# A macaron transformer block on one core: the ring of fetched expert rows gets eight places instead of four

## What is computed

```python
x = x + 0.5 * ffn(layernorm(x), gate_w, gate_up_proj, down_proj)
x = x + attn(layernorm(x), w_qkv, w_out)
x = x + 0.5 * ffn(layernorm(x), gate_w, gate_up_proj, down_proj)

def ffn(x):                       # 16 experts, each token goes to the best 2
    p = sigmoid(x @ gate_w.T); p = p / p.sum(-1)
    w, idx = top_k(p, 2);      w = w / w.sum(-1)
    # expert e: (silu(x @ gate_e) * (x @ up_e)) @ down_e, 256 -> 128 -> 256
    # out = sum of the two experts' outputs, weighted with w
```

## Time and profile before

| | |
|---|---|
| median of 3 runs | 817.87 us (816.4 to 819.97) |
| the profiled execution, whole | 817.24 us |
| its span, first to last instruction | 815.4 us |
| TensorE clock granted, mean of the span | 0.929 |
| busy, share of the span | PE 82%, PEld 65%, DVE 65%, ACT 51%, POOL 51% |
| chain that ended last, by engine | PE 62%, DVE 17%, issue 5%, DMA 4%, ACT 4%, POOL 2% |
| indirect fetches of line 1356 | 80, together 76.9 us busy on POOL |

### The profile page before, as it was taken

The page is one execution under the profiler, slowest core; times in us unless marked ns, Lnnn a source line. Parts: engine busy times, 40 slices in busy tenths (PEclk is TensorE's granted clock), DMA queues, the critical chain, the costliest instruction groups (busy, mean ns, idle before and its releaser), DMA issues.

```text
span 815.4 us, 17364 instructions
## 1 busy us (share of the span) xinstructions
PE 665.5 (82%) x5367; PEld 530.3 (65%) x5384; DVE 528.8 (65%) x1644; ACT 418.3 (51%) x1024; POOL 417.1 (51%) x557
## 2 busy tenths in 40 slices
PE   2638999887868999999999899896775656998990
PEld 2438889776746777777777566664434546887880
DVE  7888644333666888788888988855486313343678
ACT  1534566555414555555555555555564524565660
POOL 4124555555342555455555542357677674555551
PEclk9958999999978999999999999999877787999996
DMA  8793456555553444444444333246115343555979
GB/s 255 246 295 96 137 159 170 155 137 144 136 152 100 117 119 121 119 117 112 116 119 114 98 87 86 74 139 204 60 69 173 100 153 123 153 146 145 308 260 325
DMA packets 96920, 121.04 MB, mean 148 GB/s; under 512 B 12352, under 2 KB 83280, under 8 KB 96848
## 3 DMA queue, kind: packets, MB, share of 16 engines
q1 hardware_dynamic: 82992, 81.82, 33.5%
q0 software_dynamic: 13824, 38.29, 16.2%
q10 hardware_dynamic: 32, 0.02, 0.0%
HBM read 51.99 MB, written 38.34 MB: 111 GB/s over the span
## 4 chain that ended last, share of the span: by engine, by line
PE 62%; DVE 17%; issue 5%; another core or an unknown queue 4%; DMA 4%; ACT 4%; POOL 2%; SPq 2%; DVEq 0%; ACTq 0%; POOLq 0%
PE bank L1208 9%; PE bank L1516 8%; PE bank L613 6%; PE bank L1220 5%; PE bank L1523 4%; PE bank L674 4%; PE bank L635 4%; PE bank L660 4%; PE bank L694 3%; DVE mx L1020 3%; PE bank L620 3%; PE bank L1198 2%; PE bank L638 2%; PE bank L1507 2%
## 5 line engine op out<-in xcount | busy, mean ns | idle before, releaser
L525 POOL TENSOR_SCALAR_AFFINE_SELECT pr<-pr 128x512 f32<-128x512 f32 x128 | 81.4, 658 | 135.6 <-ACT pr L790 132.5
L1020 DVE TENSOR_REDUCE mx<-bank 128x2 f32<-128x512 f32 (+1 forms) x192 | 127.7, 683 | 29.6 <-PE bank L638 21.7
L790 ACT ACTIVATE pr<-bank 128x512 f32<-128x512 f32 x192 | 105.8, 603 | 40.0 <-PE bank L660 22.6
L1356 POOL DMA_INDIRECT spare<-normed,source x80 | 76.9, 962 | 89.4 <-PE bank L1507 43.6
L1166 POOL DMA_INDIRECT returned<-shared,source x80 | 77.5, 969 | 62.4 <-DVE shared L1296 41.7
L1208 PE MATMUL bank<-xeT,shared 128*128 128x128 f32 x640 | 90.0, 286 | 10.8 <-ACT xeT L1261 6.8
L1208 PEld LDWEIGHTS bank<-xeT,shared 128*128 128x128 f32 x640 | 82.7, 202 | 12.3 <-issue 12.0
L1516 PE MATMUL bank<-xeT,shared 128*128 128x128 f32 x640 | 87.6, 281 | 1.2 <-ACT xeT L1643 1.0
L1516 PEld LDWEIGHTS bank<-xeT,shared 128*128 128x128 f32 x640 | 80.6, 198 | 2.1 <-issue 2.0
L1289 DVE TENSOR_TENSOR act_rows<-bank,act_rows 128x128 f32<-128x128 f32 x80 | 23.2, 290 | 89.0 <-ACT act_rows L1277 55.3
L432 POOL DMA_INDIRECT gathered_rows<-grouped,slot x64 | 67.4, 1053 | 16.1 <-issue 12.3
(11 more groups left out here) (344 smaller groups left out, 1496.3 us busy)
## 6 DMA issues: line engine op xcount, KB each, us to landing
shared<-parts SPq DMA_DIRECT2D x154, 128.0 KB
grouped<-pr SPq DMA_DIRECT2D x80, 132.0 KB
spare<-grouped SPq DMA_DIRECT2D x80, 132.0 KB
spare<-parts SPq DMA_DIRECT2D x70, 128.0 KB
shared<-returned SPq DMA_DIRECT2D x32, 256.0 KB
normed<-shared SPq DMA_DIRECT2D x8, 512.0 KB, 3.9
wgu_sb<-_L_ffn_gate_up_proj_dram SPq DMA_DIRECT2D x8, 512.0 KB, 8.7
wd_sb<-in_L_ffn_down_proj_dram SPq DMA_DIRECT2D x8, 512.0 KB
```

The lines of the kernel that those rows point to most:

```text
L525: nc.gpsimd.affine_select(out=m, in_=m, compare_op=ALU.is_ge, fill=0.0, base=0, pattern=[[0, 4], [1, P]], channel_multiplier=-1).then_inc( ...
L790: nc.scalar.activation(dst.rearrange("p h n -> p (h n)"), bank[n % 3][:, :], ACT.Exp).then_inc(at["exp_ready"], 1)
L1020: nc.vector.tensor_reduce(mx[:, u, h0:h0 + nh], bank[3 + n % 2][:, :].rearrange("p (h k) -> p h k", h=nh), AX.X, ALU.max).then_inc(at["max ...
L1356: nc.gpsimd.indirect_dma_start(xe[r], None, normed, bass.IndirectOffsetOnAxis(source[:, j:j + 1], 0)).then_inc(xe_loaded[r], 16)
```

## The change

`AHEAD_X` = 8 replaces the four places: `xe` becomes the first 2048 columns of `spare`, with eight semaphores `xe_loaded`. The fetch of tile j waits for the transposes of tile j-8. As four of the places now lie where `wqk_in` lay, the fetch of tile 0 also waits until ACT has copied the q and k weights. PE's loop goes round eight tiles, in 8 iterations instead of 16, so that each place's address and semaphore are constants. The last block, which uses the same semaphores for the first of its 16 places, counts from the new totals. The ring of results `ye`, the loops of ACT, DVE and SP, and the place and number of the gathers are as before.

```diff
--- before.py
+++ after.py
@@ -43,6 +43,7 @@
     DUMP = TOPK * WIDE[2] * P
     ID_0 = [DUMP + (NE_T + TOPK * WIDE[1]) * P, DUMP + NE_T * P, 0]
     NK = NE_T // RING
+    AHEAD_X = 2 * RING
     LOADS = 4
     LATE = 6
     ROUNDS = NT // RING
@@ -207,7 +208,7 @@
         gathered_rows = sb("gathered_rows", [P, RING, TOPK, W])
         got = [[gathered_rows[:, r, k, :] for k in range(TOPK)] for r in range(RING)]
         before_in, source_in, passed_in = (bank[3], bank[5]), (bank[5], bank[4]), (bank[7], bank[5])
-        xe = [spare[:, (RING + r) * H:(RING + r + 1) * H] for r in range(RING)]
+        xe = [spare[:, r * H:(r + 1) * H] for r in range(AHEAD_X)]
         xeT = sb("xeT", [P, 2, HC, P])
         att = xeT[:, :, :, :].rearrange("p u c n -> p u (c n)")
         act_rows = sb("act_rows", [P, 2, 2, I])
@@ -303,10 +304,10 @@
         att_consts = sem("att_consts")
         first_block = {n: sem(f"{n}_f") for n in first_names}
         last_block = {n: sem(f"{n}_l") for n in last_names}
-        xe_loaded = [sem(f"xe_loaded{r}") for r in range(RING)]
+        xe_loaded = [sem(f"xe_loaded{r}") for r in range(AHEAD_X)]
         xl_loaded = [sem(f"xl_loaded{r}") for r in range(PLACES_X)]
         scattered = [sem(f"scattered{a}") for a in range(1, CLASSES)]
-        yl_returned = xe_loaded + [sem(f"yl_returned{r}") for r in range(RING, PLACES_Y)]
+        yl_returned = xe_loaded + [sem(f"yl_returned{r}") for r in range(AHEAD_X, PLACES_Y)]
         ye_stored = [sem(f"ye_stored{r}") for r in range(RING)]
         xn_stored = [sem(f"xn_stored{i}") for i in range(BACK)]
         late_loaded = (ye_stored + xn_stored)[0:LATE]
@@ -329,7 +330,7 @@
 
         def returns(r, n):
 
-            return 16 * (len(range(r, n, PLACES_Y)) + (NE_T // RING if r < RING else 0))
+            return 16 * (len(range(r, n, PLACES_Y)) + (NE_T // AHEAD_X if r < AHEAD_X else 0))
 
         count = [0]
 
@@ -1350,9 +1351,11 @@
 
             def fetch(j):
 
-                r = j % RING
-                if j >= RING:
-                    pool.wait_ge(s["xe_transposed"], j - RING + 1)
+                r = j % AHEAD_X
+                if j >= AHEAD_X:
+                    pool.wait_ge(s["xe_transposed"], j - AHEAD_X + 1)
+                elif j == 0:
+                    pool.wait_ge(at["wqk_ready"], 2 * HC)
                 nc.gpsimd.indirect_dma_start(xe[r], None, normed, bass.IndirectOffsetOnAxis(source[:, j:j + 1], 0)).then_inc(xe_loaded[r], 16)
 
             def stored_up_to(n):
@@ -1496,7 +1499,7 @@
                 place_tokens(k)
             passed_row(0)
 
-            body = RING
+            body = AHEAD_X
             alone = SURE - 1
             loops = (NE_T - alone - 1) // body
```

## The result

The changed kernel took 831.57 us (median of 4 runs, 826.4 to 833.09), the kernel before, on the same chip, 818.92 us (4 runs): ratio 1.015, interval 1.011 to 1.019. It is slower, by 12.7 us in the medians. The forecast was 823.5 and slower; the sign was right, and so in the main was the mechanism, but the size was half of what came.

A forecast was written before the change was run, and what follows sets the result against it. PE bounds the steady part; elsewhere POOL's back-to-back indirect DMAs delay reports of PE's work. Terms +1.9, +4.67 and -0.3 sum to +6.3 on 817.24, giving 823.5 us; range 809 to 832, the forecast alone 819.5 to 828.

The forecast's parts named there:

- the sign: Whole kernel: slower, 823.5 us against a profiled 817.24; slower was given 0.52, same 0.30, faster 0.18.
- the mechanism: First block's expert tiles: while POOL issues indirect DMAs back to back, PE's finished work is told late and everything stands.
- The wait at the head: Before the first fetch: waiting for ACT's q and k weight copies, over at 46.1 before the fetch at 55.04, costs nothing.
- the loop of eight: PE's loop over expert tiles: same instructions, half the branches, already hidden; 0, with a bound of -0.6 us.
- The start: 55 to 75 us: 15 fetches in a row cost 0, as a run of four did and DVE's routing sets the end.
- Rival C: Start: the run of 15 fetches hits DVE's routing chain, one standstill of 8 us on top, 831.5; chance 0.10.
- The pause for the list: Fetch 16, waiting for the list of all pairs: a run of at least five follows, +1.9 us, bounds 0 and 3.7.
- The first gathers: From 155.9 us: POOL's run grows from five to ten, 6.25 us more standing, 1.58 saved at gather 2: +4.67.
- the end: Last fetch of the expert tiles: issued eight tiles ahead, so the 0.3 us of waits for a fetch go: -0.3.
- Gathers 3 to 7: Later gathers among the fetches: each still costs 1.58 us as before, 6.2 us a step.
- Rival A: Stretch of the gathers: the ring is what stalls it, so more places make it faster, 811.8 to 802.3; chance 0.18.
- Rival B: Long waits come from the moment's traffic, not run length: no change, 816.9 to 818, at 817; chance 0.22.

The follow-up runs named there:

- the first experiment: The changed kernel with all its code, but the fetch of tile j waits for the transposes of tile j-4 as before: 816.48 us, ratio 0.9976 to the kernel before.

## Why the prediction was right, and where it was off

PE's first work on an expert tile, in the trace of before, bears on the second point:

```profile
60.55 1.03 PE L1507 MATMUL bank<-ident,spare 128*128 128x128 f32 x4
```

- **The wait at the head and the loop of eight: 0.** Right; the first experiment keeps both and loses nothing.
- **The start: 0, with 8 as the rival's price.** This is the step that failed: 4.3 us. I took the run of four at the start as showing that a run costs nothing here. It could not show that. The run is over at 59.33 + 0.95 = 60.28, and PE's first work on an expert tile starts only at 60.55, so there was no report of its tiles to be held. With eight places the run went on to 68.76, over PE's first tiles. It had eleven DMAs (15 had been forecast; the twelfth fetch waited for tile 3, whose report was held). Rival C had the mechanism and the place, at twice the price. The price does not follow from the length alone: the runs of five cost 5.4 us before the change and 3.0 at the list, the run of eleven 4.3. The rest of my reason for 0, that DVE sets the end here, did not cover it: DVE itself waits for ACT, and ACT for PE.
- **The pause for the list: +1.9.** The run of five came as forecast, and cost 3.0, inside the bounds of 0 and 3.7 and nearer to the row that had the same length.
- **The first gathers: +4.67, and the end: -0.3.** Run of ten in the forecast order; 4.6 us lost from tile 54 to 79 against the sum of 4.4. The single waits are shorter than the 8 to 10 us I expected, since they come in three pieces of 8.1 us together. The sum took its 6.25 us as standing still alone. Over tiles 54 to 60 idle time rose only from 4.8 to 8.1 us, and slower work at the lower clock from 2.3 to 4.5, so it is in part luck that the term came out so well. Gathers 3 to 7 cost 6.4 a step instead of 6.2.
- **Nothing between tile 14 and 54.** PE was 1.0 us quicker there.
- **Rival A (the ring frees the stretch of the gathers).** Wrong: POOL's runs got longer and PE's waits with them. **Rival B (the traffic of the moment).** Wrong on these chips: six DMAs of 4 KB did it in the steady stretch, and more traffic with pauses did not.

The forecast of 6.3 us stands against 9.2 in the profiled execution and 12.7 in the medians. Of the 2.9 us between forecast and profile, the start makes +4.3, the list +1.1, the first gathers +0.2, the steady part -1.0 and what follows tile 79 -1.8. The other 3.5 us are not settled.

The median of 831.57 lies outside the 819.5 to 828 that the forecast had for itself, and within the whole range of 809 to 832 by 0.4 us, which it owes to rival C. That it falls on C's 831.5 is chance: C's term came at 4.3 us, not 8, and the rest is spread over the list and what is not located.

And one thing was right by luck of the chip. The sum rests on a behaviour that the trace of before showed well, and that another chip does not have. There the changed kernel with six fetches more was 0.2% faster than the kernel before.

## What to carry to other kernels

A deeper ring removes waits for data; look first whether there are any, and then ask what the producer will do with its freedom, since it can issue in longer unbroken runs after every wait that it alone has. Where a trace shows an engine idle without a releaser, look at what another engine issued without a pause just then, and peg those issues one by one to the consumer's progress rather than give them more room. When a trace names no cause for a stall, measure on more than one chip before building on it.

## What the runs showed of the hardware

- On the first chip and those like it, reports of PE's products come late while POOL issues indirect DMAs 0.3 us apart: in a run of eleven up to 5.2 us, in a run of ten 3.4 to 10.5 us, the last of them 2.0 and 2.2 us after the run's end. In a run with the DMAs 0.66 us apart (1.61 from start to start) they come after 0.03 us. The measure is the start of ACT's silu against the modelled end of PE's products.
- The size of the transfers has no part in it: 128 rows of 32 bytes take POOL 0.95 us to issue like 128 rows of 1 KB, and six such DMAs held PE 7.0 us in three pieces.
- A short row is enough: after a pair of DMAs 0.3 us apart PE idled 1.46 us in one place and 0.2 to 0.8 in others, after three in a row 0.6 to 1.8.
- After the standstills at the first gathers PE's gate and up took 2.05 us instead of 1.06, the granted clock over that stretch being 0.85.
- On the second chip 21 in a row cost PE nothing (busy 25.00 of 25 us), and the kernel before takes 763.9 us instead of 811.8 to 818.9. What differs between the chips, and at which point PE's signals are held on the first, the traces do not show.
- A small write on POOL between two indirect DMAs is free: 0.14 us of it lie inside the 0.30 us.
